# A transformer-like block in one launch: softplus in two VectorE steps, the last norm and half of the dt work moved into the scan phase, GpSimd's first two dt steps behind the softmax's weighing

## What is computed

```python
x = x + L0_conv(ln_c(x))            # Mamba on 4 chunks of 64 channels, norm, projection
t = tokens(x); t = t + L0_ffn(ln_t(t))      # fp8-rounded matmul with bias
x = x + L1_conv(ln_c(image(t)))     # group norm, attention between channels, projection
t = tokens(x); t = t + L1_ffn(ln_t(t))      # mixture of 8 experts, top 2, GELU
```

```python
dt = softplus(dt_proj(x_proj(xc)) + dt_bias)
h  = exp(dt * A) * h + (dt * xc) * B     # along the 1024 tokens
y  = sum_over_states(h * C) + xc * D;  y = y * silu(z)
```

## Time and profile before

| | us |
|---|---|
| median of 3 runs | 1981.06 |
| lowest, highest | 1978.47, 1984.16 |
| profiled execution | 1983.14 |
| its span, first to last instruction | 1981.2 |
| TensorE / VectorE / ScalarE / GpSimd busy | 1528.7 / 1346.4 / 767.4 / 1166.9 |
| mean granted TensorE clock | 0.928 of full speed |

### The profile page before, as it was taken

How to read it: one execution, slowest core, us unless ns; L and a number is a source line. 1 busy time by engine, 2 the same in 40 slices (tenths; PEclk the granted TensorE clock), 3 DMA queues, 4 the chain that set the end, 5 groups by cost and what they waited for, 6 DMA issues and landing times. The chain is left out here.

```text
span 1981.2 us, 20702 instructions
## 1 busy us (share of the span) xinstructions
PE 1528.7 (77%) x5773; PEld 941.8 (48%) x5806; DVE 1346.4 (68%) x1441; ACT 767.4 (39%) x1201; POOL 1166.9 (59%) x605
## 2 busy tenths in 40 slices
PE   5467678867677886777786677767369999999997
PEld 2122224542222453222444222235258888888887
DVE  2899998579999768999867899983642222222222
ACT  6535334654442664444277353322112222222222
POOL 0699892359987038989513998930045554545543
PEclk9689999979999997999998899988579999999999
DMA  3075560146554015646202655653102222222222
GB/s 117 27 270 198 189 204 23 41 166 215 193 180 139 23 61 202 211 163 214 84 22 83 243 202 181 207 219 137 66 24 41 33 40 35 38 37 37 37 33 27
DMA packets 80697, 230.71 MB, mean 116 GB/s; under 512 B 12844, under 2 KB 31605, under 8 KB 77270
## 3 DMA queue, kind: packets, MB, share of 16 engines
q1 hardware_dynamic: 64694, 210.93, 30.6%
q0 software_dynamic: 15904, 18.66, 5.9%
HBM read 208.15 MB, written 19.82 MB: 115 GB/s over the span
## 5 line engine op out<-in xcount | busy, mean ns | idle before, releaser
L390 PE MATMUL psum<-HC_sb,ident_sb 128*128 128x512 f32 x1024 | 493.7, 606 | 65.1 <-DVE HC_sb L1362 57.4
L390 PE MATMUL psum<-experts_sb 64*128 64x512 f32 (+5 forms) x930 | 307.7, 562 | 240.6 <-DVE HC_sb L1362 149.3
L952 ACT ACTIVATE psum<-experts_sb 128x1024 f32<-128x1024 f32 x256 | 285.5, 1117 | 506.8 <-DVE experts_sb L1352 393.8
L1352 DVE TENSOR_TENSOR_SCAN experts_sb<-psum,DBX_sb 128x1024 f32<-128x1024 f32 x172 | 389.7, 2275 | 31.7 <-POOL DBX_sb L1042 30.7
L390 PEld LDWEIGHTS psum<-HC_sb,ident_sb 128*128 128x128 f32 x1024 | 190.0, 192 | 282.0 <-issue 131.8
L390 PEld LDWEIGHTS psum<-experts_sb 64*128 64x128 f32 (+5 forms) x962 | 97.9, 153 | 473.9 <-DVE HC_sb L1362 240.7
L1886 DVE TENSOR_TENSOR YS_sb<-psum_moe,b_sb 128x256 f32<-128x256 f32 x71 | 30.1, 424 | 353.5 <-PE psum_moe L1641 349.9
L1734 ACT ACTIVATE hgt_sb<-psum_moe,b_sb 128x256 f32<-128x256 f32 (+1 forms) x312 | 116.5, 456 | 381.2 <-PE psum_moe L1641 381.2
L1641 PE MATMUL psum_moe<-XGT_sb,w1s_sb 128*128 128x256 f32 (+1 forms) x1248 | 253.6, 362 | 0.0
L1641 PE MATMUL psum_moe<-experts_sb,hgt_sb 128*128 x1136 | 251.7, 379 | 0.7 <-DVE YS_sb L1886 0.7
L1618 POOL DMA_INDIRECT out<-YS_sb,scat_sb x71 | 131.7, 1855 | 203.9 <-DVE YS_sb L1890 188.7
(11 more groups left out here) (264 smaller groups left out, 1742.7 us busy)
## 6 DMA issues: line engine op xcount, KB each, us to landing
DA_sb<-bc_rows SPq DMA_DIRECT2D x128, 512.0 KB, 4.6
experts_sb<-bc_rows SPq DMA_DIRECT2D x64, 512.0 KB, 3.7
SQ_sb<-bc_rows SPq DMA_DIRECT2D x64, 512.0 KB, 4.2
X_XT_sb<-bc_rows SPq DMA_DIRECT2D x64, 512.0 KB, 5.5
experts_sb<-w1T SPq DMA_DIRECT2D x8, 1024.0 KB, 19.3
experts_sb<-w2T SPq DMA_DIRECT2D x8, 1024.0 KB, 21.3
X_sb<-x_tok SPq DMA_DIRECT2D x5, 1024.0 KB, 7.1
experts_sb<-x_tok SPq DMA_DIRECT2D x4, 1024.0 KB, 4.8
```

The source lines that it names most:

```text
L390: return nc.tensor.matmul(o, lhsT, rhs, start=start, stop=stop, **k)
L952: nc.scalar.activation(decays[i % 2], DT[:, c, :], ACT.Exp, scale=a_neg[:, s:s + 1]).then_inc(da_ready, 1)
L1352: v.tensor_tensor_scan(STATE[i % STATE_SLOTS], decays[i % 2], DRIVE[i % STATE_SLOTS], 0.0, ALU.mult, ALU.add).then_inc(h_ready, 1)
```

## The change

- **Softplus:** ScalarE takes Exp, a Ln that is shifted and scaled, Square and Relu; VectorE combines them in two steps (a product and a min with a sum) instead of five. `exp_ln` is `exp_of` and `logs_of`. The third and fourth log tiles lie where the residual's x is loaded, so that load comes later.
- **GpSimd:** `add_ffn_bias` goes (the bias is added by bf16 matmuls into the fp8 matmul's PSUM). In a gap GpSimd first waits for the weighing (`att_done`), then does the dt steps of chunks 0 and 1, then `split_bc`. The steps of chunk 2 stand behind drive 2 of the scan phase, those of chunk 3 behind drive 8. The shift of the first norm goes from VectorE to GpSimd (`first_shift`).
- **Last norm:** the gate matmul runs on the raw third residual (the mean is folded into the gate weights), the logits are scaled by 1/std afterwards. 1/std comes from Ln and Exp and one correction on VectorE (`last_rstd`, four operations of 128 x 8), the group norm's likewise. The norm itself is done by ScalarE at scan steps 4 to 7; only in the tail at the end of the front.
- **Order:** z gates stand behind decay 1 of the scan phase on ScalarE; the bc matmul is behind the dt matmuls, the third of them ahead of the group variance; the first half of norm 1's scale comes two tokens earlier and loses a multiply; the last chunk's gate, projection and skip go by halves, and TensorE's turn of y is in the scan phase. Read-outs of GpSimd are s = 2, 6, 10, 14.
- **SP:** the token store at row 8, the wait for both stores and the next image's load at row 10, the residual's load at row 13 behind all dt steps.

```diff
-POOL_READS = (3, 7, 11, 15)
+POOL_READS = (2, 6, 10, 14)
...
-SP_STEPS = 5
...
+SP_STEPS = 2
...
-        C_REP = (X1_XT[:, 0:L], X1_XT[:, L:2 * L])
+
+        def c_rep(q):
+            return T[:, q, :] if q < 2 else X1_XT[:, q % 2 * L:(q % 2 + 1) * L]
 
         def log_tile(c):
-            return SZ[:, c, :] if c + 1 < NC else U4
...
-                load_x(b)
                 store_bc(b)
-                load_b(b, 0)
-                load_b(b, 1)
+                for i in range(3):
+                    load_b(b, i)
                 spread_bc(b)
                 store_x3(b - 1)
-                store_tm(b - 1)
                 sp.wait_ge(gate_done, b)
+                sp.sem_inc(tokens_there, 1)
                 for i in range(2, NI):
-                    load_b(b, i)
-                    if i == POOL_READS[0]:
+                    if i >= 3:
+                        load_b(b, i)
+                    if i == TOKENS_AT:
+                        store_tm(b - 1)
+                    if i == NEXT_AT:
                         sp.wait_ge(stored, b * 32)
+                        sp.sem_inc(tokens_there, 1)
+                    load_c(b, i)
+                    if i == NEXT_AT:
                         load_next(b + 1)
-                    load_c(b, i)
+                    if i == X_AT:
+                        sp.wait_ge(dt_done, b * NC + NC)
+                        sp.sem_inc(tokens_there, 1)
+                        load_x(b)
...
             def dt_linear(b, c):
-                if c == NC - 1:
-                    pe.wait_ge(brow_ready, b + 1)
-                    pe.wait_ge(bc_copy, b + 1)
-                else:
-                    pe.wait_ge(xc_done, (b * NC + c // 2 * 2) * NH + (4 if c else 3))
...
             def bc_linear(b):
-                pe.wait_ge(xc_done, (b + 1) * NC * NH)
+                pe.wait_ge(sp_relu, b * NC + 3)
...
                     for n in (2 * k, 2 * k + 1):
+                        at = psum[:, k, (n % 2) * C:(n % 2 + 1) * C]
+                        mm(at, ones_b[:, :], FB_PARTS[:, :], True, False)
                         for c in range(CT):
-                            i = mm(psum[:, k, (n % 2) * C:(n % 2 + 1) * C], QBC[:, c, n * P:(n + 1) * P], ffn_q[:, c, :],
-                                   c == 0, c == CT - 1)
+                            i = mm(at, QBC[:, c, n * P:(n + 1) * P], ffn_q[:, c, :], False, c == CT - 1)
...
             def tm_turn(p, h):
-                pe.wait_ge(tm_done, p * NB + (4 * h + 4))
-                if h:
-                    pe.wait_ge(x3_done, p * 4 + 4)
+                pe.wait_ge(x3_done, p * 4 + (2 + 2 * h))
                 for c in range(CT):
                     for n in range(4 * h, 4 * h + 4):
-                        i = turn(psum[:, TM_BANKS[h] + c, (n % 4) * P:(n % 4 + 1) * P], TM[:, n, c * P:(c + 1) * P])
+                        i = turn(psum[:, TM_BANKS[h] + c, (n % 4) * P:(n % 4 + 1) * P], X2[:, n, c * P:(c + 1) * P])
                 i.then_inc(tm_turned, 1)
...
+                if go_on:
+                    dt_linear(b, 2)
                 group_var(p)
-                if go_on:
-                    bc_linear(b)
                 hc_turn(p, 1)
                 scores(p)
                 if go_on:
-                    dt_linear(b, 2)
                     dt_linear(b, 3)
+                    bc_linear(b)
                 attend(p)
-                if go_on:
-                    z_pair(b, 0)
                 out_linear(p)
-                if go_on:
-                    z_pair(b, 1)
                 tm_turn(p, 0)
                 tm_turn(p, 1)
                 gate(p)
+                if go_on:
+                    z_pair(b, 0)
+                    z_pair(b, 1)
                 pe.wait_ge(gate_done, p + 1)
 
             def scans(b):
@@ -682,15 +700,22 @@
...
+            def exp_of(b, c):
                 n = b * NC + c
                 e = DT[:, c, :]
                 act.wait_ge(sp_abs, n + 1)
                 nc.scalar.activation(e, e, ACT.Exp, scale=-1.0).then_inc(sp_exp, 1)
                 act.wait_ge(sp_exp, n + 1)
+                nc.scalar.activation(log_tile(c), e, ACT.Ln, scale=LOG_SCALE, bias=log_shift[:, :]).then_inc(sp_log, 1)
+
+            def logs_of(b, c):
+                n = b * NC + c
                 if c >= 2:
                     act.wait_ge(sp_step, b * (NC * SP_STEPS) + ((c - 1) * SP_STEPS))
-                nc.scalar.activation(square_tile(c), e, ACT.Square, bias=series_shift[:, :]).then_inc(sp_sq, 1)
-                nc.scalar.activation(log_tile(c), e, ACT.Ln, bias=1.0).then_inc(sp_ln, 1)
+                nc.scalar.activation(square_tile(c), DT[:, c, :], ACT.Square, scale=SERIES_SCALE,
+                                     bias=series_shift[:, :]).then_inc(sp_sq, 1)
+                act.wait_ge(sp_log, n + 1)
+                nc.scalar.activation(log_tile(c), log_tile(c), ACT.Relu).then_inc(sp_ln, 1)
...
+            def token_rsqrt(p):
...
+                    act.wait_ge(mv_done[3], p * 2 + h + 1)
+                    nc.scalar.activation(token_std[:, 3, m], token_mv[:, 3, m, 1], ACT.Ln, bias=eps5[:, :]).then_inc(log_done, 1)
+                    act.wait_ge(log_done, p * 3 + (h + 2))
+                    nc.scalar.activation(token_rs[:, 3, m], token_std[:, 3, m], ACT.Exp, scale=-0.5).then_inc(std_done[3], 1)
...
+            def last_norm(p, tiles):
+                act.wait_ge(rsqrt_step, p * 8 + 8)
+                for n in tiles:
+                    nc.scalar.activation(TM[:, n, :], X2[:, n, :], ACT.Identity, scale=token_rs[:, 3, n:n + 1],
+                                         bias=token_nb[:, 3, n:n + 1]).then_inc(tm_done, 1)
...
                 q_copy(p, 0)
@@ -902,39 +953,38 @@
                 q_copy(p, 1)
                 if go_on:
                     read_dt(b, 1)
-                token_sqrt(2, p, eps6)
-                token_norm(2, p, XT, X2, h_done)
+                for h in range(NH):
+                    token_sqrt(2, p, h, eps6[:, :])
...
                 if go_on:
+                    exp_of(b, 0)
+                    logs_of(b, 0)
+                    silu_x(b, 1)
                     nc.scalar.preload_act_table_set(EXP_LN)
-                    exp_ln(b, 0)
-                    silu_x(b, 1)
-                    nc.scalar.preload_act_table_set(SQRT)
...
-                nc.scalar.preload_act_table_set(EXP_LN)
+                scores(p)
+                if go_on:
+                    logs_of(b, 1)
+                    read_dt(b, 2)
+                softmax(p)
+                if go_on:
+                    read_dt(b, 3)
+                attend(p)
                 if go_on:
                     read_bc(b)
-                scores(p)
-                if go_on:
-                    exp_ln(b, 1)
-                softmax(p)
-                if go_on:
-                    read_dt(b, 2)
-                attend(p)
-                if go_on:
-                    read_dt(b, 3)
-                    exp_ln(b, 2)
-                    exp_ln(b, 3)
-                    silu_z(b, 0)
-                nc.scalar.preload_act_table_set(SQRT)
-                token_sqrt(3, p, eps5)
-                token_norm(3, p, TM, X2, tm_done)
+                    for c in range(2, NC):
+                        exp_of(b, c)
+                        logs_of(b, c)
                 tm_copy(p, 0)
+                token_rsqrt(p)
                 tm_copy(p, 1)
-                if go_on:
-                    silu_z(b, 1)
+                if not go_on:
+                    last_norm(p, range(NB))
 
...
                     decay(i)
+                    if i == 1 and after:
+                        silu_z(b, 0)
+                        silu_z(b, 1)
+                        nc.scalar.preload_act_table_set(EXP_LN)
+                    if 4 <= i < 8 and after:
+                        last_norm(b - 1, (2 * i - 8, 2 * i - 7))
...
-            def between(p, b):
-                add_ffn_bias(p)
-                if b is not None:
-                    steps_of_dt(b, 0)
-                    split_bc(b)
-                    steps_of_dt(b, 1)
-                    steps_of_dt(b, 2)
-                    steps_of_dt(b, 3)
+            def between(b):
+                pool.wait_ge(att_done, b * 2)
+                steps_of_dt(b, 0)
+                steps_of_dt(b, 1)
+                split_bc(b)
+
+            def first_shift(b):
+                pool.wait_ge(f_small, b * 2 + 1)
+                nc.gpsimd.tensor_tensor(f_nb[:, :], f_neg[:, :], f_rs[:, :], ALU.mult).then_inc(f_small, 1)
...
                     drive(i)
+                    if i == STATE_SLOTS - 1:
+                        steps_of_dt(b, 2)
+                    if i == 8:
+                        steps_of_dt(b, 3)
+                    if i == FIRST_AT + 2 * NB + NB // 2 + 1:
+                        first_shift(b + 1)
...
-            def log1p(b, c, steps=range(SP_STEPS)):
+
+            def log1p(b, c):
                 n = b * NC + c
...
```

(63 more changed lines are left out.)

231 lines of the change are left out of this document (123 added, 108 removed).

## The result

The changed kernel took **1926.77 us** (median of 4 runs, 1925.99 to 1928.82) beside 1979.76 us for the kernel before: ratio 0.9731, 95% interval 0.9712 to 0.9749, that is 53 us faster. Run once more beside later experiments it took 1923.88 us (5 runs), ratio 0.9717 (0.9704 to 0.9730); I compare the experiments with this second run. The forecast was 1914, the range 1886 to 1945, so the sign and the range held; the point was 10 to 13 us too low (against 1923.88 and 1926.77). The terms were off by more than the sum.

What follows compares the result with a forecast made beforehand. VectorE was taken to bound the scan phases, a chain jumping between engines the gaps; scan phases −8, gaps −38, start −16.5 and tail −4.4 sum to −67, so 1981 − 67 = 1914 us, range 1886 to 1945.

Steps and rivals of the forecast that it cites:

- Start, −16.5: Before the first scan: fewer VectorE softplus steps and an earlier row request bring it from 102.88 to 86.4 us; bounds 10 to 19.
- Tail, −4.4: After the last scan: halves at phase end, norm 1's order and the gate ahead of the last norm save 4.4 us.
- Gaps, −38: Three gaps between scan phases: each loses 2.8 + 4.3 + 5.5 + 0.2 = 12.8 us.
- the others stand like L1097 until the third drive is done: Gap, weighing to logits: two rescale products slip in before the first drive, the rest wait; logits 31.2 us behind weighing, −5.5.
- rival A: GpSimd lets VectorE in between its instructions, so the four products cost what they do alone: 1893 or 1880 us; chance 0.2.
- Scan phases, −8: Four scan phases together: −23 us from moving the small product, +15.3 from dt-step stalls, nothing for the rest.
- The fourth dt step: Scan phases, GpSimd behind drive 8: VectorE stalls about 2.3 us at scan 9; phase 0 costs 8.4 with the third step.
- ScalarE's last norm at scans 4 to 7: Scan phases: eight 0.5 us norm instructions fit beside the decays, costing nothing; if late, the token store would hold row loads.
- rival C: Scan phases: SP's queue starves the drives; 25 us of stall in each phase gives 2014 us, slower; chance 0.04.
- Rival B: GpSimd's string is worse: a gap gives 7, start 10, tail 2, and stalls are 5 us a phase: 1948 us; chance 0.2.
- D: No gain since the softplus steps were hidden anyway and only the ends count: 1970 to 1980 us; chance 0.04.
- signs of being wrong: GpSimd idling long before drive 0 of a later phase, drives waiting for DMA, or a gap under 107 us.

Runs made afterwards that it cites:

- again: The changed kernel run once more with no edit, beside later experiments: 1923.88 us, ratio 0.9717 to the kernel before.
- an earlier gap end: Against the changed kernel, GpSimd's dt step of chunk 0 stands ahead of the softmax weighing instead of behind it: 1920.42 us, ratio 0.9688.
- four edits: Changed kernel with GpSimd's shift two steps later, z gates ahead of decay 0, last norm's products ahead of chunk 2's logarithm, chunk 0's dt step ahead of weighing: 1899.53 us.

## Why the prediction was right or wrong

The total came within 13 us of the point because two large misses partly cancel: the gaps gave 13 us more than forecast, and the scan phases took 25 to 28 us more. So the near hit is in part luck, and the terms have to be judged one by one.

*Start, −16.5.* Measured −17.2 and −18.0, but the times inside it came out otherwise. SP's queue, GpSimd and VectorE in the changed kernel:

```profile
75.74 0.98 SPq L336 DMA_DIRECT2D DA_sb<-bc_rows  x2
```
```profile
80.50 4.65 POOL L1089 TENSOR_TENSOR DBX_sb<-DA_sb,experts_sb 128x1024 f32<-128x1024 f32 x2 [7.64 <-DMA DA_sb<-bc_rows]
```
```profile
85.64 4.47 DVE L1400 TENSOR_TENSOR_SCAN experts_sb<-psum,DBX_sb 128x1024 f32<-128x1024 f32 x2 [7.92 <-ACT psum L1002]
```

The row was asked for at 75.74, 3.8 us earlier than the 79.5 that I had, and drive 0 was done by about 82.9. The first scan then waited for ScalarE's first decay, behind z gates and a table load, which my sum didn't have. The two misses nearly cancel, so the point here was partly luck. The three added softplus steps alone cost 9.0 there.

*Tail, −4.4.* Measured −5.6 and −7.5, where the bounds were 1 and 7. It is the difference of two larger terms. The logits come 11.2 and 13.7 us earlier behind the last scan, with a granted clock of 0.84 and 0.88 in that stretch against 0.81 before, and no run says how much of it is the clock's. From the logits to the end it takes 5.7 and 6.2 us longer: in the tail the last norm (4.0 us) and the store of the tokens stand at and behind the logits now (store asked for at 1343.59, logits at 1341.93; before at 1396.16, logits at 1401.73), and all engines wait for that store. My term left the longer end out. The experts don't blur the reading: from the logits to the end the changed kernel and all its variants took 584.0 to 585.4 us.

*Gaps, −38.* Measured −51.0 and −50.8, 16.5 to 17.5 each instead of 12.8. Against the end of the last scan, in the second gap: quantizing starts 4.3 us earlier (667.02 − 639.33 = 27.7, now 23.4), the diagonal product 4.4, the weighing ends 8.8 earlier (forecast 7.1), the logits 14.6 (forecast 12.6), the first scan 17.0. Why the weighing came 1.7 us earlier than forecast is open; the granted clock of this gap was 0.93 against 0.89. From weighing to logits I had 31.2 us and it took 31.0, but not by the mechanism. VectorE in the second gap, then GpSimd:

```profile
706.75 3.25 DVE L1157 SCALAR_TENSOR_TENSOR experts_sb<-experts_sb 128x1024 f32<-128x1024 f32 x1
710.04 2.19 DVE L1351 SCALAR_TENSOR_TENSOR token_fix_sb<-token_mv_sb,token_rs_sb 128x8 f32<-128x8 f32 x1
712.27 2.26 DVE L1353 SCALAR_TENSOR_TENSOR token_fix_sb<-token_fix_sb,token_rs_sb 128x8 f32<-128x8 f32 x1
714.56 2.26 DVE L1355 SCALAR_TENSOR_TENSOR token_rs_sb<-token_fix_sb,token_rs_sb 128x8 f32<-128x8 f32 x1
716.86 0.17 DVE L1357 SCALAR_TENSOR_TENSOR token_nb_sb<-token_mv_sb,token_rs_sb 128x8 f32<-128x8 f32 x1
```
```profile
705.60 6.61 POOL L1089 TENSOR_TENSOR DBX_sb<-DA_sb,experts_sb 128x1024 f32<-128x1024 f32 x2
712.17 2.33 POOL L1089 TENSOR_TENSOR SQ_sb<-experts_sb 128x1024 f32<-128x1024 f32 x1
714.47 2.33 POOL L1056 TENSOR_TENSOR experts_sb<-experts_sb 128x1024 f32<-128x1024 f32 x1
```

GpSimd runs from 705.60 to 716.80 without a pause, and still each product ends with one of its instructions (712.21, 714.50, 716.80). My step "the others stand like L1097 until the third drive is done" is wrong. VectorE gets in between, as in rival A, though not for free as A had it: the third drive ended 28.3 us behind the weighing (I had 31), the products came 23.8 behind it (I had 21), and three waits of one instruction each cost 6.7 us, which brought the logits to my number by luck. (I had also counted ten series steps in this stretch of the kernel before; its timeline has eleven, which no term uses.) Another 2.2 us of the larger gain are from the logits to the first scan (4.7 us now, 7.14 before, forecast 6.9). The trace has the two softplus steps of the last chunk there, 3.24 and 1.22 us, and 0.29 us more; the first scan doesn't wait for a drive any more, and the third drive is done 2.7 us ahead of the logits. It isn't that the z gates left the gap: with the gates ahead of decay 0 the same stretch took 4.7 us too.

The Trainium skill (SBUF — State Buffer, section "SBUF: two separate sides") has the shared ports locked for a whole instruction, and the other side blocked meanwhile. These three products agree with it, at 2.2 us each. The 5.75 us of L1097, two and a half instructions, don't follow from that rule, and no run here reproduced them.

*Scan phases, −8.* Measured +19.7 and +16.6: this step failed, by 25 to 28 us. Of the 19.7 us, by the intervals of all four phases: the stretch with the small product −15.3 (I had −23), scans 4 to 16 with the fourth dt step and the late rows +18.8 (I had 15.3), scans 1 to 4 with read-out 0 +9.7 (again: +6.3; I had nothing), scans 16 to 32 and 40 to 56 +6.5 (I had nothing). Point by point:
- "The small product goes to GpSimd, where it waits for nobody: −5.75, four times." VectorE's busy time did fall by 5.1 a phase. But GpSimd waited 4.98 us for the reciprocal, and 1.9 us a phase (0.7 in the first) came back as stalls of scans 36 and 37. The run with the shift later shows it. And the saving came with the product's new place and the new read-out steps anyway, as the run with the shift back on VectorE shows.
- The fourth dt step: I had 2.3 us at scan 9; it was 3.0, and the 8.4 of the first phase came out at 6.0 (its first 16 scans took 53.4 us; before they took 48.5, and with the shifted read-out they would take 47.4 without a stall). The size was nearly right, but in the later phases the cause is double.
- ScalarE's last norm at scans 4 to 7, and SP's waits with rows asked for four drives ahead: I had nothing for both, and that is a cost. Every instruction of the norm fits, but SP's store stands behind the last of them, 15.4 us, and the rows of the next steps behind the store. I had named just this condition and did not work out its times: decay 7 can't start before scan 5 is done, and SP is at row 8 already when drive 4 is done. In the changed kernel drive 11 waits 1.4 to 2.7 us for its row; where the fourth dt step doesn't cover the rest, drives 9 and 11 wait 2.81 and 3.25 us. That is rival C's mechanism at a small size: not 25 us a phase, some 3. A run without SP's wait wasn't made, so its worth alone stays open.
- The z gates behind decay 1 had no term in the scan phases at all, only in the gap. They cost 1.6 to 4.0 us at read-out 0 in three phases, and the run with the gates ahead has no such wait. In sum that is 9.1 us in the first profiled run and 5.3 in the second, and my sum had nothing for it.
- Scans 16 to 32 take at least 1.3 us more in every variant, of which 0.57 is a wait for a drive at scan 29; no run here took it away.

Rival B (string worse) and D (softplus hidden) are excluded by the gaps and by the run with three more steps. Two of my signs of being wrong came true: the first gap is under 107 us (105.4), which is wrong in the direction of more gain, and drives wait for DMA in the later phases (drive 11).

## What to carry to other kernels

A step moved from a gap into a stage with a full engine isn't free because it fits in time: list what the other queues do behind it (the store behind the norm, the rows behind the store, the C row behind the gates), with the time at which each is asked for. A wait that an engine far ahead meets costs its lead, and the stall shows up steps later at another engine; two steps' distance removed it here and took 6.4 us off the stretch behind it. And try edits together: an earlier gap end gained 3.5 us by itself, and four edits that gave 2 to 7 us each, 18 in sum, gave 24 together (which pair of them makes the difference wasn't run; the intervals point at the early dt step and the gates).

## What the hardware showed that I had not expected

- One and the same tiny product of VectorE (128 x 8, two operands in SBUF) took 5.75 us in the kernel before, and 0.17 us two scans later, in a pause of GpSimd; 0.20 to 0.23 us when it came just ahead of a boundary between two of GpSimd's instructions. Products of the same size in the gap, written as scalar_tensor_tensor, took 2.2 us where they came just behind such a boundary. What made the first one miss two boundaries is open, and its other form (tensor_tensor) hasn't been ruled out.
- Where two-operand instructions of both engines alternate, GpSimd slows as well: two drives took 6.61 us instead of 4.7 beside VectorE steps of 3.00 and 3.25, which take 1.22 alone.
